# Cross attention: the keys of a tile are projected a step ahead, and VectorE rotates first in a step

## The chip, the cores and the metric

The kernel runs on one core of one Trainium2 chip. The metric is the device time of one execution in microseconds (us), here the median of several runs. PE is TensorE, PEld its weight loads, DVE VectorE, ACT ScalarE, POOL GpSimd, SP the engine that issues most of the DMAs.

## What is computed

A decoder layer on 16 sequences of 112 tokens, width 512, in float32: self attention, cross attention over 375 context tokens and the 112 of the sequence itself, and a mixture of experts. The change lies in the cross attention, which does this (cut from the reference):

```python
kv_in = jnp.concatenate([context_hidden, draft_hidden], axis=1)      # 375 + 112 = 487 rows
k = (kv_in @ Wk.T).reshape(bsz, total_len, KVH, HD)                  # 4 key heads of 128
v = (kv_in @ Wv.T).reshape(bsz, total_len, KVH, HD).transpose(0, 2, 1, 3)
k = _rms_norm(k, k_norm_w).transpose(0, 2, 1, 3)
q = _rope(q, draft_position_ids)
k = _rope(k, full_position_ids)
k = jnp.repeat(k, N_REP, axis=1)                                     # 16 query heads, 4 to a key head
scores = jnp.einsum('bhqd,bhkd->bhqk', q, k) * SCALE
probs = jax.nn.softmax(scores, axis=-1)
attn = jnp.einsum('bhqk,bhkd->bhqd', probs, v)
```

## The kernel before

`cross_attention` is one block in which each engine runs a program of its own, its order written out by hand; semaphores tie the programs together. `wait(eng, event, b, n)` holds an engine until the n-th event of batch b has happened. The 487 rows of keys and values are handled as four tiles i = 0 to 3: three of 125 context rows, one of the 112 rows of the sequence. The 16 query heads are four groups i = 0 to 3 of four heads j, one to a key head. So a batch is four *steps*, and step (b, i) does two things at once: the softmax of group i of batch b, and the projection of tile i of batch b + 1.

TensorE's operations are `score` (L2030, one head's scores into `ca_ps_s`, two buffers), `weigh` (L2046, probabilities times values of the group in front, into `ca_ps_o`), `keys` and `values` (`mm3`, L75 to L77, 12 matmuls each in three-part precision, into `ca_ps_p`), `turn` (L2037, four transposes of a head's probabilities into `ca_ps_t`) and `turn_k` (L2021, four transposes of a tile's finished keys into `ca_ps_r`).

Projected keys go through four engines. ScalarE squares them (`square`, L2092). VectorE multiplies them with the tables of sine and cosine (`rotate`, L2188 and L2191) into `k1` and `k2`, and sums the squares (`squares`, L2198, L2201). GpSimd adds the two products (L1958), takes the power -1/2 of the mean square (L1960) and scales the keys (L1964), and then makes the low part of the next context tile (`low`, L1952; ScalarE's `high`, L2085, makes the high part). TensorE turns the keys, and ScalarE copies them to `kT` (`keep_k`, L2097). The `keys` of a tile wait for its low part and for the rotation of the tile in front, the `rotate` for the turning of the tile in front.

The softmax of a head is `score`, `maximum` (VectorE, L2206), `exp` (ScalarE, L2112), `divide` (VectorE, L2211 and L2213), `turn`, `copy_pT` (ScalarE, L2119) and, in the next step, `weigh` and `copy_o` (ScalarE, L2124). The first score of a batch waits for `kT` of all four tiles.

`batches` runs `start` four times for the first batch (the preparation, with nothing beside it), then `step` 64 times, of which the last four (b = 15) project nothing. Steps of batches 2 to 13 are a hardware loop. `more` says that there is a next batch to project. The DMAs of the stage are SP's: `load` (x and tables of batch b + 2), `load_ctx` (context, L1891, once the low part of the last tile is made), `load_q` and `store`.

Of the kernel before, what the change touches and what calls it, by code (L numbers as in the profile page):

```python
# [1771 lines left out]
def cross_attention(nc, ahead_of, ctxT, xT_hi, xT_lo, tables, qT_src, oT):  # L1772
# [6 lines left out]
    with ctx:  # L1779
# [84 lines left out]
        def begun(b, i):  # L1864

            return not isinstance(b, int) or b or i

        def before(b, i):

            return (b, i - 1) if i else (b - 1, 3)

        @block.sync
        def _(sp):
            for i in range(2):
                o_put[i].open(sp)

            def load(b, h, par):
                cols = bass.ds(b * S, S)
                if not isinstance(b, int) or b > 1:  # L1880
                    wait(sp, v_mm, b, -5)
                    carry(sp, b, ticks)
                    wait(sp, k_rot, b, -5)
                    carry(sp, b, ticks)
                sp.dma_start(xh[par][:, :, :].bitcast(F32), xT_hi[:, :, cols]).then_inc(x_in[par].sem, 16)
                sp.dma_start(xl[par][:, :, :].bitcast(F32), xT_lo[:, :, cols]).then_inc(x_in[par].sem, 16)
                sp.dma_start(tab[par][:, :, :, :], tables[b]).then_inc(tab_in[par].sem, 16)

            def load_ctx(b):
                wait(sp, c_lo_ready, b, -1)  # L1890
                sp.dma_start(c_raw[:, :, :], ctxT[b]).then_inc(c_in.sem, 16)  # L1891

            def load_q(b, i):
                if not isinstance(b, int) or b or i > 1:
                    wait(sp, scored, b, (i - 1) * HQ - 1)
                sp.dma_start(qT[i % 2][:, :, :], qT_src[:, i * HQ:(i + 1) * HQ, bass.ds(b * S, S)])\
                    .then_inc(q_in[i % 2].sem, 16)

            def store(b, i):
                wait(sp, o_ready, b, i)  # L1900
                carry(sp, b, ticks)
                sp.dma_start(oT[:, i * HQ:(i + 1) * HQ, bass.ds(b * S, S)], ov[i % 2][:, :, :])\
                    .then_inc(o_put[i % 2].sem, 16)

            def body(b, h, par, first=False, more=1):

                load_q(b, 2)
                if not first:
                    store(b - 1, 3)  # L1910
                if more > 1:
                    load(b + 2, h + 1, par)
                load_q(b, 3)
                store(b, 0)
                if more > 1:
                    load_ctx(b + 2)
                if more:
                    load_q(b + 1, 0)
                store(b, 1)
                if more:  # L1920
                    load_q(b + 1, 1)
                store(b, 2)

            load(0, 0, 0)
            load_q(0, 0)
            load_q(0, 1)
            load(1, 0, 1)
            load_ctx(1)
            body(0, 0, 0, first=True, more=2)
            body(1, 0, 1, more=2)  # L1930
            with sp.Fori(1, B // 2 - 1) as h:
                for par in range(2):
                    body(h * 2 + par, h, par, more=2)
            body(B - 2, B // 2 - 1, 0, more=1)
            body(B - 1, B // 2 - 1, 1, more=0)
            store(B - 1, 3)
            for i in range(2):
                sp.wait_ge(o_put[i].sem, o_put[i].at(B - 1, 1))
# [39 lines left out]
        def _(pe):  # L1978
# [13 lines left out]
            def keys(b, h, i, par):  # L1992
                if first(b) and i == 0:
                    pe.wait_ge(w_lo_ready, 1)
                m, a_hi, a_lo = operands(b, i, par)
                if i == 3:
                    wait(pe, x_in[par], h, 1)
                else:
                    wait(pe, c_lo_ready, b, i)
                wait(pe, k_rot, b, i - 1)  # L2000
                for k in range(KD):
                    mm = mm3(pe, ps_p[0][0:m, :], a_hi[:, k, :], a_lo[:, k, :], w_hi[:, 0, k, :], w_lo[:, 0, k, :],
                             k == 0, k == KD - 1)
                mm.then_inc(k_mm.sem, 1)

            def values(b, i, par):
                if first(b) and i == 0:
                    pe.wait_ge(w_lo_ready, 2)
                m, a_hi, a_lo = operands(b, i, par)
                wait(pe, v_ready, b, i - 1)  # L2010
                for k in range(KD):
                    mm = mm3(pe, ps_p[1][0:m, :], a_hi[:, k, :], a_lo[:, k, :], w_hi[:, 1, k, :], w_lo[:, 1, k, :],
                             k == 0, k == KD - 1)
                mm.then_inc(v_mm.sem, 1)

            def turn_k(b, i):
                m = M[i]
                wait(pe, k_normed, b, i)
                wait(pe, kT_ready, b, i - 1)
                for j in range(KVH):  # L2020
                    mm = pe.transpose(ps_r[:, j * m:(j + 1) * m], k1[0:m, j * HD:(j + 1) * HD], ident[0:m, 0:m])  # L2021
                mm.then_inc(k_turned.sem, 1)
# [17 lines left out]
            def weigh(b, i, par):  # L2040
# [6 lines left out]
                                   start=(t == 0), stop=(t == 3))  # L2047
                mm.then_inc(pv.sem, 1)

            def start(b, i, par):  # L2050
                keys(b, 0, i, par)
                values(b, i, par)
                turn_k(b, i)

            def step(b, h, i, par, more):
                score(b, h, i, 0, par)
                score(b, h, i, 1, par)
                if begun(b, i):
                    pb, pi = before(b, i)
                    weigh(pb, pi, par if i else 1 - par)  # L2060
                if more:
                    keys(b + 1, h + par, i, 1 - par)
                turn(b, i, 0)
                turn(b, i, 1)
                score(b, h, i, 2, par)
                score(b, h, i, 3, par)
                if more:
                    values(b + 1, i, 1 - par)
                turn(b, i, 2)
                turn(b, i, 3)  # L2070
                if more:
                    turn_k(b + 1, i)

            batches(pe, start, step)
            weigh(B - 1, 3, 1)

        @block.scalar
        def _(act):
# [7 lines left out]
                    .then_inc(c_hi_ready.sem, 1)  # L2086

            def square(b, i):
                m = M[i]
                wait(act, k_mm, b, i)  # L2090
                wait(act, k_sum, b, 2 * i - 2)
                act.activation(sq[0:m, :], ps_p[0][0:m, :], ACT.Square).then_inc(k_sq.sem, 1)  # L2092
# [8 lines left out]
            def keep_v(b, i, par):  # L2101
                m = M[i]
                wait(act, v_mm, b, i)
                if not isinstance(b, int) or b > 1:
                    wait(act, pv, b, -5)
                act.activation(v[par][0:m, i, :], ps_p[1][0:m, :], ACT.Copy).then_inc(v_ready.sem, 1)
# [25 lines left out]
            def split(n):  # L2132
                act.wait_ge(w_in[n], 16)
                act.activation(w_hi[:, n, :, :], w_raw[:, n, :, :], ACT.Copy).then_inc(w_hi_ready, 1)

            def start(b, i, par):
                square(b, i)
                next_high(b, i, par)
                keep_v(b, i, par)
                keep_k(b, i, par)  # L2140

            def step(b, h, i, par, more):
                nb, npar = b + 1, 1 - par
                exp(b, i, 0)
                exp(b, i, 1)
                if begun(b, i):
                    copy_o(*before(b, i))
                if more:
                    square(nb, i)
                copy_pT(b, i, 0)  # L2150
                copy_pT(b, i, 1)
                exp(b, i, 2)
                exp(b, i, 3)
                if more:
                    keep_v(nb, i, npar)
                    next_high(nb, i, npar)
                copy_pT(b, i, 2)
                copy_pT(b, i, 3)
                if more:
                    keep_k(nb, i, npar)  # L2160

            k_sq.open(act)
            kT_ready.open(act)
# [4 lines left out]
            split(0)  # L2168
            high(0, 0, 0)
            split(1)  # L2170
            batches(act, start, step)
            copy_o(B - 1, 3)

        @block.vector
        def _(dve):
# [46 lines left out]
                squares(b, i)  # L2222

            def step(b, h, i, par, more):
                maximum(b, i, 0)
                maximum(b, i, 1)
                divide(b, i, 0)
                divide(b, i, 1)
                if more:
                    rotate(b + 1, h + par, i, 1 - par)  # L2230
                maximum(b, i, 2)
                maximum(b, i, 3)
                if more:
                    squares(b + 1, i)
                divide(b, i, 2)
                divide(b, i, 3)

# [489 lines left out]
```

## Time and profile before

| what | value |
|---|---|
| median of 3 runs | 2579.57 us (2574.31 to 2584.58) |
| the profiled execution | 2563.0 us, of which the span from first to last instruction is 2561.3 us |
| mean granted clock of TensorE | 0.941 of full speed |
| busy over the span | PE 86%, PEld 65%, DVE 52%, ACT 40%, POOL 31% |
| first score of the cross attention | at 1074.0 us |
| last score of the cross attention | at 1999.1 us |

The shares are means over stages with different limits, so the stage from some 1030 to 2005 us is read by itself.
### The profile page before, as it was taken

The numbers are of one execution on the slowest core, as the hardware profiler recorded it, in microseconds if no ns is written. First come the engines' busy times: TensorE is split into PE (matmuls) and PEld (weight loads), VectorE is DVE, ScalarE is ACT, GpSimd is POOL, SyncE is SP. The second block draws the span as 40 slices with busy tenths as digits, with TensorE's granted clock in tenths as the row PEclk, the third lists the DMA queues.
The fourth block names the chain that finished last, engine by engine and source line by source line (L and its number), as shares of the span: only waits on it lengthen the run. The fifth ranks groups of instructions, "written<-read, shape, count | busy, mean of one in ns | idle before, by whom it ended". The sixth has DMA issues, their size and how long they took to land. (4 is left out here: it accounts for less than half of the span.)

```text
span 2561.3 us, 35639 instructions
## 1 busy us (share of the span) xinstructions
PE 2201.1 (86%) x10448; PEld 1668.9 (65%) x10448; DVE 1333.2 (52%) x2902; ACT 1032.6 (40%) x2200; POOL 787.7 (31%) x818
## 2 busy tenths in 40 slices
PE   5699999975999986799999999999999799839991
PEld 3588888854777765566666666666665577627771
DVE  3535555547666766344444444444444555535553
ACT  2323333324434444244544544444455422125660
POOL 2400000004455556322322322322331011136664
PEclk9899999987999998799999999999999899959996
DMA  7621221142444444222222211222221533235336
GB/s 278 167 69 37 66 64 33 37 174 71 131 136 119 125 131 154 62 63 57 64 68 56 63 56 56 63 56 56 61 58 37 161 103 98 62 137 177 107 100 193
DMA packets 291586, 243.77 MB, mean 95 GB/s; under 512 B 148034, under 2 KB 255026, under 8 KB 288562
## 3 DMA queue, kind: packets, MB, share of 16 engines
q1 hardware_dynamic: 271426, 194.38, 25.6%
q10 hardware_dynamic: 13584, 30.02, 3.2%
q0 software_dynamic: 6496, 18.37, 2.6%
q8 instruction: 41, 0.67, 0.1%
q14 instruction: 39, 0.32, 0.0%
HBM read 149.31 MB, written 93.42 MB: 95 GB/s over the span
## 5 line engine op out<-in xcount | busy, mean ns | idle before, releaser
L2206 DVE TENSOR_REDUCE ca_down<-ca_ps_s 112x1 f32<-112x487 f32 x256 | 164.6, 661 | 210.6 <-PE ca_ps_s L2030 207.9
L1958 POOL TENSOR_TENSOR ca_k<-ca_k 125x512 f32<-125x512 f32 x64 | 82.5, 1290 | 606.8 <-DVE ca_k L2191 606.8
L2030 PE MATMUL ca_ps_s<-ca_kT,ca_qT 128*112 128x487 f32 x512 | 233.3, 577 | 13.0 <-ACT ca_kT L2097 10.0
L2112 ACT ACTIVATE ca_prob<-ca_ps_s,ca_down 112x487 f32<-112x487 f32 x256 | 169.7, 666 | 151.7 <-DVE ca_down L2206 147.7
L75 PE MATMUL out_ps_y<-out_w_hi,out_o_hi 128*128 128x512 f32 x448 | 190.6, 425 | 36.4 <-DVE out_w_lo L1288 18.4
L2046 PE MATMUL ca_ps_o<-ca_pT,ca_v 125*128 125x448 f32 (+1 forms) x512 | 203.2, 539 | 0.6 <-ACT ca_pT L2119 0.6
L75 PE MATMUL ca_ps_p<-ca_w_hi,ca_c_hi 128*125 128x512 f32 x384 | 187.6, 489 | 12.3 <-POOL ca_c_lo L1952 12.3
L2188 DVE TENSOR_TENSOR ca_k<-ca_ps_p,ca_tab 125x512 f32<-125x512 f32 x64 | 44.3, 692 | 289.0 <-ACT ca_sq L2092 289.0
L76 PE MATMUL out_ps_y<-out_w_lo,out_o_hi 128*128 128x512 f32 x448 | 183.2, 409 | 0.0
L77 PE MATMUL out_ps_y<-out_w_hi,out_o_lo 128*128 128x512 f32 x448 | 182.5, 407 | 0.0
L2046 PEld LDWEIGHTS ca_ps_o<-ca_pT,ca_v 125*128 125x128 f32 (+1 forms) x512 | 97.2, 190 | 100.9 <-issue 100.1
L77 PE MATMUL ca_ps_p<-ca_w_hi,ca_c_lo 128*125 128x512 f32 x384 | 153.7, 400 | 0.0
L76 PE MATMUL ca_ps_p<-ca_w_lo,ca_c_hi 128*125 128x512 f32 x384 | 153.5, 400 | 0.0
L2037 PEld LDWEIGHTS ca_ps_t<-ca_ident,ca_prob 112*125 112x125 f32 x1024 | 131.8, 188 | 23.1 <-DVE ca_prob L2213 10.2
L599 POOL COPY sa_val<-lat_v 112x128 f32<-112x128 f32 (+1 forms) x64 | 18.7, 294 | 411.0 <-PE sa_ps_o L656 410.7
L2037 PE MATMUL ca_ps_t<-ca_ident,ca_prob 112*125 112x112 f32 x1024 | 132.7, 272 | 6.3 <-DVE ca_prob L2213 5.7
L2030 PEld LDWEIGHTS ca_ps_s<-ca_kT,ca_qT 128*112 128x112 f32 x512 | 81.0, 177 | 76.4 <-issue 76.4
L75 PEld LDWEIGHTS out_ps_y<-out_w_hi,out_o_hi 128*128 128x128 f32 x448 | 89.8, 200 | 59.1 <-issue 33.1
L2119 ACT ACTIVATE ca_pT<-ca_ps_t 125x448 f32<-125x448 f32 x256 | 125.0, 544 | 3.8 <-PE ca_ps_t L2037 3.8
L2213 DVE TENSOR_SCALAR ca_prob<-ca_prob,ca_inv 112x487 f32<-112x487 f32 x256 | 121.2, 474 | 9.0
L75 PE MATMUL sa_ps_q<-sa_xh,qf_hi 128*128 128x448 f32 (+1 forms) x256 | 115.7, 452 | 8.5 <-DMA sa_xl<-x0T_lo 8.5
L707 ACT ACTIVATE sa_ov<-sa_ps_o 128x448 f32<-128x448 f32 x64 | 34.9, 546 | 194.8 <-PE sa_ps_o L656 187.8
(291 smaller groups left out, 5603.1 us busy)
## 6 DMA issues: line engine op xcount, KB each, us to landing
self_outT<-sa_ov SPq DMA_DIRECT2D x64, 224.0 KB, 2.4
out_o_raw<-self_outT SPq DMA_DIRECT2D x56, 256.0 KB, 3.0
cross_qT<-out_qt SPq DMA_DIRECT2D x56, 256.0 KB, 2.5
ca_qT<-cross_qT SPq DMA_DIRECT2D x64, 224.0 KB, 2.8
cross_outT<-ca_ov SPq DMA_DIRECT2D x64, 224.0 KB, 3.0
out_o_raw<-cross_outT SPq DMA_DIRECT2D x56, 256.0 KB, 3.1
ffn_raw<-in_expert_w SPq DMA_DIRECT2D x8, 1536.0 KB, 6.8
ca_c_first<-in_ctxT SPq DMA_DIRECT2D x15, 750.0 KB, 4.2
```

The source lines that it names most:

```text
L75: pe.matmul(out, a_hi, b_hi, start=start, stop=False)
L76: pe.matmul(out, a_hi, b_lo, start=False, stop=False)
L77: return pe.matmul(out, a_lo, b_hi, start=False, stop=stop)
L1958: pool.tensor_tensor(k1[0:m, :], k1[0:m, :], k2[0:m, :], ALU.add).then_inc(k_added.sem, 1)
L2030: pe.matmul(ps_s[j % 2][:, :], qT[i % 2][:, j, :], kT[par][:, i, :], start=True, stop=True).then_inc(scored.sem, 1)
L2037: mm = pe.transpose(ps_t[j % 2][0:CT, t, :], prob[j][:, t * CT:(t + 1) * CT], ident[0:S, 0:S])
L2046: mm = pe.matmul(ps_o[:, :, :], v[par][0:M[t], t, i * HD:(i + 1) * HD], pT[i % 2][0:M[t], t, :, :], start=(t == 0), stop=(t == 3))
L2112: act.activation(prob[j][:, 0:KV], ps_s[j % 2][:, :], ACT.Exp, bias=down[:, j:j + 1], accum_out=total[:, j:j + 1]).then_inc(exped.sem, 1)
L2119: act.activation(pT[i % 2][0:CT, :, j, :], ps_t[j % 2][0:CT, :, :], ACT.Copy).then_inc(pT_ready.sem, 1)
L2188: dve.tensor_tensor(h4(k1[0:m, :]), h4(ps), over_heads(tab[par][0:m, i, 0, :], HQ), ALU.mult)
L2206: dve.tensor_reduce(down[:, j:j + 1], ps_s[j % 2][:, :], AX.X, ALU.max, negate=True).then_inc(maxed.sem, 1)
L2213: dve.tensor_scalar(prob[j][:, 0:KV], prob[j][:, 0:KV], inv[:, j:j + 1], None, ALU.mult).then_inc(probs.sem, 1)
```

## The change

In a step TensorE now does the `values` where it did the `keys`, turns the keys right behind the scores of heads 2 and 3, and projects the keys of the tile that is turned in the *next* step (`next_keys`) in front of the last two `turn`s. ScalarE's and VectorE's programs follow: `square` moves behind `keep_k` in the second half, `rotate` to the front of the step, `squares` between the maxima and the divisions of the first half. `further` says whether there is a tile left for `next_keys`.

```diff
+        def further(b, i):
+            return not isinstance(b, int) or b + (2 if i == 3 else 1) < B
...
+            def next_keys(b, h, i, par):
+                if i < 3:
+                    keys(b, h, i + 1, par)
+                else:
+                    keys(b + 1, h + par, 0, 1 - par)
+
             def start(b, i, par):
-                keys(b, 0, i, par)
                 values(b, i, par)
+                next_keys(b, 0, i, par)
                 turn_k(b, i)
 
             def step(b, h, i, par, more):
...
                     weigh(pb, pi, par if i else 1 - par)
                 if more:
-                    keys(b + 1, h + par, i, 1 - par)
+                    values(b + 1, i, 1 - par)
                 turn(b, i, 0)
                 turn(b, i, 1)
                 score(b, h, i, 2, par)
                 score(b, h, i, 3, par)
                 if more:
-                    values(b + 1, i, 1 - par)
+                    turn_k(b + 1, i)
+                if further(b, i):
+                    next_keys(b + 1, h + par, i, 1 - par)
                 turn(b, i, 2)
                 turn(b, i, 3)
-                if more:
-                    turn_k(b + 1, i)
-
+
+            keys(0, 0, 0, 0)
             batches(pe, start, step)
...
             def square(b, i):
-                m = M[i]
+                m = M[i % 4]
...
             def start(b, i, par):
-                square(b, i)
                 next_high(b, i, par)
                 keep_v(b, i, par)
+                square(b, i + 1)
                 keep_k(b, i, par)
 
             def step(b, h, i, par, more):
                 nb, npar = b + 1, 1 - par
                 exp(b, i, 0)
                 exp(b, i, 1)
+                if more:
+                    next_high(nb, i, npar)
                 if begun(b, i):
                     copy_o(*before(b, i))
                 if more:
-                    square(nb, i)
+                    keep_v(nb, i, npar)
                 copy_pT(b, i, 0)
                 copy_pT(b, i, 1)
                 exp(b, i, 2)
                 exp(b, i, 3)
                 if more:
-                    keep_v(nb, i, npar)
-                    next_high(nb, i, npar)
+                    keep_k(nb, i, npar)
+                if further(b, i):
+                    square(nb, i + 1)
                 copy_pT(b, i, 2)
                 copy_pT(b, i, 3)
-                if more:
-                    keep_k(nb, i, npar)
...
+            square(0, 0)
             batches(act, start, step)
...
             def step(b, h, i, par, more):
+                if more:
+                    rotate(b + 1, h + par, i, 1 - par)
                 maximum(b, i, 0)
                 maximum(b, i, 1)
+                if more:
+                    squares(b + 1, i)
                 divide(b, i, 0)
                 divide(b, i, 1)
-                if more:
-                    rotate(b + 1, h + par, i, 1 - par)
                 maximum(b, i, 2)
                 maximum(b, i, 3)
-                if more:
-                    squares(b + 1, i)
                 divide(b, i, 2)
                 divide(b, i, 3)
```

## Rows read from the trace of the kernel before

**Rows 1.** Stretches of the preparation and of one batch: length, busy time of each engine.

```profile
core 0: us, PE busy (x) PEld busy (x) DVE busy (x) ACT busy (x) POOL busy (x), PEclk, DMA share, GB/s
1026.00:1074.00 48.00, 33.18 (x112) 24.25 (x112) 15.20 (x22) 9.89 (x17) 18.95 (x16) 0.78 0.18 57
1133.00:1192.00 59.00, 57.23 (x241) 38.11 (x241) 27.94 (x68) 29.11 (x67) 17.23 (x15) 1.00 0.23 61
```

**Rows 2.** Waits of TensorE's matmuls, 1074 to 1962: total us, times, longest.

```profile
PE ca_ps_r L2021 <- POOL ca_k L1964: 19.4, 60, 0.6
PE ca_ps_s L2030 <- ACT ca_kT L2097: 10.0, 12, 0.9
```

**Rows 3.** Waits of all engines, 1074 to 1962: the weight loads' one.

```profile
PEld ca_ps_r L2021 <- POOL ca_k L1964: 30.1, 60, 0.7
```

**Rows 4.** Time line of the weight loads through one step.

```profile
1502.98 0.28 PEld L2030 LDWEIGHTS ca_ps_s<-ca_kT,ca_qT 128*112 128x112 f32 x2
...
1504.32 0.19 PEld L2046 LDWEIGHTS ca_ps_o<-ca_pT,ca_v 125*128 125x128 f32 x1 [0.24 <-issue]
...
1507.36 0.19 PEld L75 LDWEIGHTS ca_ps_p<-ca_w_hi,ca_c_hi 128*125 128x125 f32 x1 [0.19 <-issue]
...
1510.28 1.07 PEld L2037 LDWEIGHTS ca_ps_t<-ca_ident,ca_prob 112*125 112x125 f32 x8
1511.28 0.28 PEld L2030 LDWEIGHTS ca_ps_s<-ca_kT,ca_qT 128*112 128x112 f32 x2
...
1512.60 0.19 PEld L75 LDWEIGHTS ca_ps_p<-ca_w_hi,ca_c_hi 128*125 128x125 f32 x1 [0.23 <-issue]
1513.02 0.18 PEld L76 LDWEIGHTS ca_ps_p<-ca_w_lo,ca_c_hi 128*125 128x125 f32 x1 [0.23 <-issue]
...
1515.56 1.07 PEld L2037 LDWEIGHTS ca_ps_t<-ca_ident,ca_prob 112*125 112x125 f32 x8
1517.11 0.41 PEld L2021 LDWEIGHTS ca_ps_r<-ca_ident,ca_k 125*128 125x128 f32 x4 [0.48 <-POOL ca_k L1964]
1517.49 0.28 PEld L2030 LDWEIGHTS ca_ps_s<-ca_kT,ca_qT 128*112 128x112 f32 x2
```

**Rows 5.** The same at the boundary of two batches.

```profile
1486.78 0.39 PEld L2021 LDWEIGHTS ca_ps_r<-ca_ident,ca_k 112*128 112x128 f32 x4 [0.46 <-POOL ca_k L1964]
1488.21 0.27 PEld L2030 LDWEIGHTS ca_ps_s<-ca_kT,ca_qT 128*112 128x112 f32 x2 [1.04 <-issue]
```

**Rows 6.** The same: first loads of step (0, 0) and of step (15, 0).

```profile
1074.04 0.45 PEld L2030 LDWEIGHTS ca_ps_s<-ca_kT,ca_qT 128*112 128x112 f32 x2 [0.86 <-issue]
...
1961.99 0.27 PEld L2030 LDWEIGHTS ca_ps_s<-ca_kT,ca_qT 128*112 128x112 f32 x2 [0.86 <-issue]
```

**Rows 7.** Time line of the other engines in the step of rows 4.

```profile
1504.11 0.67 DVE L2206 TENSOR_REDUCE ca_down<-ca_ps_s 112x1 f32<-112x487 f32 x1 [2.79 <-PE ca_ps_s L2030]
...
1506.61 0.47 DVE L2213 TENSOR_SCALAR ca_prob<-ca_prob,ca_inv 112x487 f32<-112x487 f32 x1
...
1510.79 0.60 ACT L2092 ACTIVATE ca_sq<-ca_ps_p 125x512 f32<-125x512 f32 x1 [2.21 <-PE ca_ps_p L77]
...
1511.28 0.97 ACT L2119 ACTIVATE ca_pT<-ca_ps_t 125x448 f32<-125x448 f32 x2
...
1511.42 0.69 DVE L2188 TENSOR_TENSOR ca_k<-ca_ps_p,ca_tab 125x512 f32<-125x512 f32 x1 [4.33 <-ACT ca_sq L2092]
...
1512.69 1.23 DVE L2206 TENSOR_REDUCE ca_down<-ca_ps_s 112x1 f32<-112x487 f32 x2
1512.85 1.28 POOL L1958 TENSOR_TENSOR ca_k<-ca_k 125x512 f32<-125x512 f32 x1 [9.19 <-DVE ca_k L2191]
...
1514.80 1.14 POOL L1960 TENSOR_TENSOR ca_k_rstd<-ca_ssum,ca_minus_half 125x4 f32<-125x4 f32 x1 [0.66 <-DVE ca_ssum L2201]
...
1516.01 1.04 POOL L1964 TENSOR_TENSOR ca_k<-ca_k,ca_k_rstd 125x512 f32<-125x512 f32 x1
...
1517.17 1.16 POOL L1952 TENSOR_TENSOR ca_c_lo<-ca_c_first,ca_c_hi 128x500 fp32r<-128x500 f32 x1
```

**Rows 8.** Time line of the preparation: tile 2 is turned, tile 3 rotated.

```profile
1062.12 0.42 PEld L2021 LDWEIGHTS ca_ps_r<-ca_ident,ca_k 125*128 125x128 f32 x4 [3.31 <-POOL ca_k L1964]
...
1067.79 0.69 DVE L2188 TENSOR_TENSOR ca_k<-ca_ps_p,ca_tab 112x512 f32<-112x512 f32 x1 [7.93 <-ACT ca_sq L2092]
```

**Rows 9.** Time line of the matmuls in the last batch.

```profile
1970.83 1.51 PE L2037 MATMUL ca_ps_t<-ca_ident,ca_prob 112*125 112x112 f32 x8 [1.44 <-DVE ca_prob L2213]
```

## The prediction

> **What bounds the kernel now.** I read the table of stretches first, to see which engine fills the stage that the diff touches. In a stretch of one batch of the cross attention TensorE is busy 57.2 of 59.0 us at a granted clock of 1.00 (2.4 GHz), while VectorE, ScalarE and GpSimd are busy about half of it or less [rows 1]. So TensorE sets the time, and only its few idle moments can be won. The chain that ended last says nothing here: it covers only the end of the kernel.
>
> Next the waits of TensorE over the 60 steps that project a tile. As matmuls they come to 19.4 us before the turning of the keys (60 times, for GpSimd's scaled keys) and 10.0 us before the first score of a batch (12 times seen, for ScalarE's copy `kT`) [rows 2]. As weight loads the first is 30.1 us [rows 3]. The two do not agree, so I went to the weight loads in order of time, which show when each group is let in. I call the groups of a step S (scores), W (`weigh`), K (`keys`), V (`values`), T (`turn`), R (`turn_k`). Today's order is S W K T S V T R.
>
> From first load to first load of the next group [rows 4]: S 1.34 (1502.98 to 1504.32), W 3.04, K 2.92, T 1.00, S 1.32, V 2.96, T 1.55, R 0.38. The two T's do the same work, yet the one in front of R takes 0.55 us more, and 0.48 of that is shown as R's wait for `ca_k`. So the row hides some 0.07 us: unhindered, the next group's loads begin 1.00 us after T's first, not 1.07. At the batch boundary R to S takes 1.43 us (1486.78 to 1488.21) instead of 0.38 [rows 5]: 1.05 us for a wait shown as 0.83 among the matmuls.
>
> **Part 1: `turn_k` in the middle of the step, its keys projected a step earlier.** Take T's load in the second half as 0. Today ScalarE's square starts 0.51 behind T's load (1510.28 to 1510.79), VectorE's rotation 1.14 behind and is over at about 2.5; GpSimd then adds 1.28, takes the root 1.14, scales 1.04 and the keys are ready at about 6.8, or 17.05 on the clock of the rows; R follows at 17.11 [rows 4, 7]. In the new order K stands in front of the last T. Square at 0.51 and rotation 1.14 to 2.41 keep their distances, since VectorE has nothing in front of the rotation; the add is over at 3.75. VectorE then does two maxima (0.67 each) and the sum of squares (0.68 and 0.17 as row 7 prices neither: from the page of the time line) to 4.6, the root ends at 5.8, the scaling at 6.9. R now comes after T 1.00, S 1.33, W 3.04, V 2.92, T 1.00, S 1.32, that is 10.6 us. It has 3.7 us to spare, so R's wait goes: 60 times (0.50 + 0.07) = 34.2, from 30.1/60 = 0.50. I round to **35 us**, as the boundary steps hide a little more.
>
> **Part 2: `kT_ready` at the batch boundary.** `keep_k` of tile 3 now lies before K and T, over 3 us ahead of the next S. 15 boundaries (the first behind the preparation) times 1.05 us: **16 us**. Together 51 us.
>
> By the matmuls' idle time alone it would be 19.4 + 15 x 0.83 = 32 us. I take the 51, because start to start of the loads includes the refilling of the array. The Trainium skill, Perfetto Trace Analysis, section Identifying the Most-Contended Engine, says that matmul busy time is no good measure of the distance to the bound, since pipelined instructions look smaller in the trace; by that rule the smaller sum is the one to distrust, and the rows agree with it (1.05 against 0.83 us).
>
> **Part 3: new neighbours in TensorE's queue.** V behind W costs what K behind W costs, 2.92. R behind S must wait for S's last pass: 0.42 (as the first load of V behind S, 1512.60 to 1513.02) plus three loads at 0.10, 0.70. K behind R then has no long pass in front of it: 2.96 less (0.42 - 0.19) = 2.73 with a load of 0.19 bare, or 2.64 if it hides behind R. R + K is 3.34 to 3.43, against 0.38 + 2.96 = 3.34 for R and V today. Cost 0 to 0.09 us a step, 0 to 5.4 in all. No row shows this succession; nothing excludes a cost twice as large, nor a small gain of the 0.07 above. I take 0.045: **+2.7 us**.
>
> **Part 4: VectorE and ScalarE.** Rotating first delays the first maximum: its score comes 1.13 us behind S's load (1502.98 to 1504.11), 2.13 on the scale above, and VectorE is free at 2.41; the `squares` in front of `divide` add 0.85. `divide` 1 was over at 1507.08, 4.1 behind S's load; it moves to about 5.0, and T needs it 7.3 behind S's load. Cover 2.3 us, cost nothing; if the cover were gone each 0.1 us would be 6 us. In the second half the rotation and `squares` go away, so `divide` 2 and 3 come 0.3 to 1 us earlier, while T comes later. On ScalarE `next_high`, `copy_o`, `keep_v` lie under V; `keep_k` under K. The square lies in front of the last two `copy_pT`, as it does in the first half today, where they end 1.97 us behind T's load (1510.28 to 1512.25). W's load comes at 2.33. **The smallest cover is here, 0.36 us**, less the time of a semaphore. Today the second pair has `keep_v` and `high` in front, but R and its wait behind T.
>
> **Part 5: loads and GpSimd.** No DMA is added or moved, and SP's queue keeps its order. `low` follows the scaling and ends at about 8.1; K needs it at 11.3: 3.2 us to spare. The context of the next batch is requested when `low` of tile 2 is done, now some 8 us earlier in its step, and is needed two steps later. Cost nothing.
>
> **Part 6: the ends.** In the preparation each tile's chain of square, rotation, GpSimd and `low` sets the pace; K of tile 1 and 2 waits for `low` as before. K of tile 3 now overlaps GpSimd's work on tile 2: today the turning of tile 2 starts at 1062.12 and the rotation of tile 3 only at 1067.79 [rows 8]; with K already done it can start at about 1063, some 4.5 us earlier. Against that `turn_k` of tile 3 queues behind `low` (1.16) and K of the next batch (2.7 us, or up to twice that, since the mean granted clock of the preparation is 0.78 [rows 1]). Net -1 to +2, taken as +0.5. The last projecting step loses its K (2.7 us) and exposes the wait of T for `divide` as the last batch has it, 1.44 [rows 9]: -1.3.
>
> **Sum.** -35 - 16 + 2.7 + 0.5 - 1.3 = **-49 us**. Check: the 60 steps took 1961.99 - 1074.04 = 887.95 us [rows 6], 14.80 each; without waits a step is 1.33 + 3.04 + 2.92 + 1.00 + 1.32 + 3.34..3.43 + 1.00 = 13.95 to 14.04, or 837 to 842 for 60, which is 46 to 51 less. The profiled execution took 2563.0 us by its own time (span 2561.3), the median of the runs is 2579.57, 0.6% above; the saving is of the same work, so I carry it over: 2514 for a profile like this one, and **2530.5** as the median.
>
> **Rivals.** (a) *Only the visible idle time comes back*: the refilling is paid elsewhere, for example at R behind S. 32 - 5.4 gives about -27: 2553. For it: that succession is in no row. Against: the check of the sum. (b) *W takes over the wait*, as `copy_pT` comes late behind the square. If it is late by 0.4 us (0.36 of cover gone and as much again), 60 times, 24 of the 49 are lost: 2554. For it the thin cover; against it that the same three instructions take 1.97 us in the first half in every step seen. (c) *Nothing changes*, because a wait of full size appears elsewhere, such as T for `divide`: it needs VectorE 2.3 us later than worked out, and then 0.8 us a step: 2580. (d) *Slower*: GpSimd's chain becomes the bound. The loop K, square, rotation, add, root, scaling, `low`, next K is 2.7 + 8.1 = 10.8 us against 14.0. It stalls from +3.2 us, and is slower than today from +4.0. If GpSimd's four instructions (4.6 us) took double beside the maxima and divisions that they now fall on, the loop is 15.4 us, 0.6 above today: +37, 2616. Against: the add already runs beside maxima today in 1.28 us, the root beside divisions in 1.14.
>
> **How the numbers follow.** My forecast 0.75; (a) 0.09; (b) 0.07; (c) 0.05; (d) 0.03; 0.01 for more gain than forecast. Some 0.5% (13 us) is what a measurement can tell: the three runs lie from 2574.31 to 2584.58. Forecast, (a) and (b) lie beyond it: faster 0.92, same 0.05, slower 0.03. Forecast alone: 2520 to 2542 (Part 3 from -4 to +11, the ends 3, the runs 5). The range that holds 8 in 10 reaches down to 2518 and, to take in most of (a) and (b), up to 2552.
>
> **What would show it.** In the new profile: no wait of the matmuls of `ca_ps_r` for `ca_k`, nor of `ca_ps_s` for `ca_kT`; TensorE over 98% busy in a stretch of one batch at clock 1.00; steps of 14.0 us; R's load 0.42 us behind S's last, K's T 2.7 behind K. (b) would show as `ca_ps_o` waiting for `ca_pT`, (c) as `ca_ps_t` waiting for `ca_prob` in the steps that project, (d) as `ca_ps_p` waiting for `ca_c_lo`. The forecast is wrong if any of these is more than a few us, or if the granted clock of the stage falls below 1.00.

## The result, and the profile after

The changed kernel takes 2522.49 us (median of 5 runs, 2519.65 to 2526.26) against 2576.06 us (5 runs, 2572.50 to 2584.58): a ratio of 0.978, 95% interval 0.9764 to 0.9796. That is 53.6 us less by the medians; 49 were forecast, from 2579.57 us, the median of the first three runs, to 2530.5. The measured 2522.5 lies in the range of 2518 to 2552, 8.0 us below the forecast: 3.5 of them come from the base, which is lower with five runs, and the rest from the larger saving.

The first view is the stretch of one batch, which answers to [rows 1]. The columns are the length, the busy time of PE, PEld, DVE, ACT and POOL, then TensorE's granted clock.

```profile
1133.00:1192.00 59.00, 59.00 (x252) 39.77 (x251) 28.95 (x71) 30.01 (x69) 19.80 (x18) 1.00 0.23 62
```

TensorE is busy in all of the 59 us, at clock 1.00. The waits of its matmuls from 1077 to 1900 us, which were 19.4 us for `ca_k` and 10.0 us for `ca_kT` before [rows 2], are down to a single line:

```profile
PE ca_ps_s L2035 <- issue: 0.8, 1, 0.8
```

The time line of the weight loads through one step answers to [rows 4]. It begins with the T in front of the step, and only the first loads of the groups are shown.

```profile
1506.26 1.08 PEld L2042 LDWEIGHTS ca_ps_t<-ca_ident,ca_prob 112*125 112x125 f32 x8
1507.27 0.28 PEld L2035 LDWEIGHTS ca_ps_s<-ca_kT,ca_qT 128*112 128x112 f32 x2
...
1508.59 0.19 PEld L2051 LDWEIGHTS ca_ps_o<-ca_pT,ca_v 125*128 125x128 f32 x1 [0.23 <-issue]
...
1511.64 0.17 PEld L75 LDWEIGHTS ca_ps_p<-ca_w_hi,ca_xh 128*112 128x112 f32 x1 [0.19 <-issue]
...
1514.56 1.07 PEld L2042 LDWEIGHTS ca_ps_t<-ca_ident,ca_prob 112*125 112x125 f32 x8
1515.55 0.28 PEld L2035 LDWEIGHTS ca_ps_s<-ca_kT,ca_qT 128*112 128x112 f32 x2
...
1516.88 0.14 PEld L2026 LDWEIGHTS ca_ps_r<-ca_ident,ca_k 112*128 112x128 f32 x1 [0.23 <-issue]
1517.29 0.33 PEld L2026 LDWEIGHTS ca_ps_r<-ca_ident,ca_k 112*128 112x128 f32 x3 [0.27 <-issue]
1517.58 0.19 PEld L75 LDWEIGHTS ca_ps_p<-ca_w_hi,ca_c_hi 128*125 128x125 f32 x1
...
1520.24 1.08 PEld L2042 LDWEIGHTS ca_ps_t<-ca_ident,ca_prob 112*125 112x125 f32 x8
1521.23 0.28 PEld L2035 LDWEIGHTS ca_ps_s<-ca_kT,ca_qT 128*112 128x112 f32 x2
```

From S to S it is 13.96 us (1507.27 to 1521.23), against 14.51 in the step of [rows 4]. R's first load stands 0.41 us in front of the others, as it was let in under the last pass of S, and R and K together take 3.36 us here (1516.88 to 1520.24) and 3.38 in the mean of the 58 steps between the first and the last, against 0.38 + 2.96 for R and V before.

The other engines in the same step answer to [rows 7]:

```profile
1506.78 0.60 ACT L2104 ACTIVATE ca_sq<-ca_ps_p 112x512 f32<-112x512 f32 x1 [1.36 <-PE ca_ps_p L77]
...
1507.27 0.97 ACT L2131 ACTIVATE ca_pT<-ca_ps_t 125x448 f32<-125x448 f32 x2
1507.41 0.69 DVE L2202 TENSOR_TENSOR ca_k<-ca_ps_p,ca_tab 112x512 f32<-112x512 f32 x1 [1.76 <-ACT ca_sq L2104]
...
1509.82 0.68 DVE L2212 TENSOR_REDUCE ca_ssum<-ca_sq 112x4 f32<-112x512 f32 x1
...
1510.53 0.17 DVE L2215 TENSOR_SCALAR ca_ssum<-ca_ssum 112x4 f32<-112x4 f32 x1
...
1510.78 1.14 POOL L1965 TENSOR_TENSOR ca_k_rstd<-ca_ssum,ca_minus_half 112x4 f32<-112x4 f32 x1 [0.68 <-DVE ca_ssum L2215]
...
1512.00 1.04 POOL L1969 TENSOR_TENSOR ca_k<-ca_k,ca_k_rstd 112x512 f32<-112x512 f32 x1
...
1513.00 1.17 POOL L1957 TENSOR_TENSOR ca_c_lo<-ca_c_first,ca_c_hi 128x500 fp32r<-128x500 f32 x1
```

Behind T's first load at 1506.26 the square comes at 0.52, the rotation at 1.15, and the scaling ends at 6.8, `low` at 7.9. R is loaded at 10.6. GpSimd's root stands idle for 0.68 us until VectorE's sum of squares is there, which matters in experiments 4 and 7. (The 0.68 and 0.17 us that the prediction takes in Part 1 for the sum of squares and its scaling are the two VectorE lines in the middle.)

Last, the first loads of step (0, 0) and of step (15, 0), which answer to [rows 6]:

```profile
1076.54 0.27 PEld L2035 LDWEIGHTS ca_ps_s<-ca_kT,ca_qT 128*112 128x112 f32 x2 [0.96 <-issue]
...
1911.83 0.28 PEld L2035 LDWEIGHTS ca_ps_s<-ca_kT,ca_qT 128*112 128x112 f32 x2
```

The 60 steps took 835.3 us instead of 887.95, 52.7 less. From the first `keys` to the last `weigh` the stage takes 923.3 us (1029.78 to 1953.07) instead of 974.9 (1028.33 to 2003.22), 51.6 less. The profiled executions themselves are only 36.7 us apart (2563.0 and 2526.3), which the first experiment looks into.

### The profile page after: what moved, and what is told of

Its sections match the earlier page's. It is cut to its first block and busy times, and to the rows that moved or that the text cites. A ratio compares the mean times of both kernels' runs of the same rounds, so it can differ in the third digit from the quotient of the medians.

```text
span 2524.6 us, 35645 instructions
## 1 busy us (share of the span) xinstructions
PE 2182.0 (86%) x10448; PEld 1661.2 (66%) x10448; DVE 1332.6 (53%) x2902; ACT 1030.3 (41%) x2200; POOL 785.3 (31%) x818
## 5 line engine op out<-in xcount | busy, mean ns | idle before, releaser
L75 PE MATMUL ca_ps_p<-ca_w_hi,ca_c_hi 128*125 128x512 f32 x384 | 174.1, 453 | 23.1 <-POOL ca_c_lo L1957 23.1
```

What stands on the lines that cost most here:

```text
L75: pe.matmul(out, a_hi, b_hi, start=start, stop=False)
```

## The experiments

The base of all but the first is the changed kernel; times are medians. Experiments 1, 2, 3 and 8 shared 15 runs of the kernel before, 2575.45 us; experiments 4 to 7 shared 7, on another chip, 2569.93 us. So a difference of medians between one of 4 to 7 and the changed kernel (2522.49, beside 2576.06) may come out up to 6 us too small, and there the stage decides. The numbers of the stage come from the weight loads of each run's profile, read as above.

### 1. The kernel before once more

The unchanged kernel.

> The kernel before, unchanged, to learn what its profile varies by behind the cross attention. In the first profile the time from the last `weigh` (2003.22 us) to the end of the span was 558.1 us; in the changed kernel it was 571.5 us (2524.6 - 1953.07). Theory A: this is variation from execution to execution, since no instruction there changed; a second profile of the kernel before shows the cross attention again as 887.9 us from the first score of step (0, 0) to that of (15, 0), but the rest behind it some 5 to 15 us longer than 558. Rival B: the changed kernel leaves the stages behind in a worse state (clock), so the kernel before repeats 558 within 2 us.

2575.76 us, ratio 1.0001 (0.9987 to 1.0015). The two profiles of it agree in the stage to some hundredths: 974.87 us against 974.89, and these are the first loads of steps (0, 0) and (15, 0), 887.97 us apart:

```profile
1077.82 0.45 PEld L2030 LDWEIGHTS ca_ps_s<-ca_kT,ca_qT 128*112 128x112 f32 x2 [0.86 <-issue]
...
1965.79 0.27 PEld L2030 LDWEIGHTS ca_ps_s<-ca_kT,ca_qT 128*112 128x112 f32 x2 [0.86 <-issue]
```

What varies lies outside: from the last `weigh` to the end 558.1 us in the first profile and 560.3 in the second, and the first `keys` of the stage came at 1028.3 and at 1032.2. That is 2.2 us, less than the 5 to 15 of theory A and a little more than B's 2. The profiles of experiments 2 to 8, all of the changed kernel's kind, have 562.2 to 567.5 us behind the stage (565.9 and 567.5 in experiments 7 and 4), so the 571.5 of the changed kernel's profile is the longest end of all. Both profiles of the kernel before were fast executions of it (2563.0 and 2569.0 against a median of 2576), and the changed kernel's was the slowest of its five (2526.26). The medians show no cost behind the stage: less the stage, the kernel before leaves 1601.2 us (2576.06 - 974.89) and the changed kernel 1599.2 (2522.49 - 923.29). What makes an end long or short stays open. The saving is to be read from the stage (51.6) and from the medians (53.6), not from one pair of profiles (36.7).

### 2. `turn_k` back at the end of the step

```diff
-                if more:
-                    turn_k(b + 1, i)
                 if further(b, i):
                     next_keys(b + 1, h + par, i, 1 - par)
                 turn(b, i, 2)
                 turn(b, i, 3)
+                if more:
+                    turn_k(b + 1, i)
```

ScalarE's `keep_k` moves behind its last `copy_pT` as well.

> The changed kernel with `turn_k` back at the end of the step, behind the last two `turn`s, while the keys are still projected a step ahead. This keeps part 1 (the turning no longer waits for GpSimd, 35 us) and undoes part 2 (the wait for `kT` at the batch boundary). Theory A, loads counted start to start: 15 boundaries at 1.05 us, 16 us more than the changed kernel, some 2539 against 2522.5. Rival B, matmul idle time counted: 12 to 15 times 0.83, 10 to 12 us, 2534. Rival C: the boundary wait was only a consequence of the late keys and is gone with them, 2522. The step without boundary stays 14.0 us in A and B.

2542.05 us, ratio 0.9871 (0.9852 to 0.9891): 19.6 more than the changed kernel. Steps inside a batch take 14.0 us, the last of a batch 15.0 to 15.1. So the wait for `kT` is a cost of its own, not a consequence of the late keys, and it costs 1.0 to 1.15 us at a boundary. The matmuls' waits from 1080 to 1900 us show less:

```profile
PE ca_ps_s L2035 <- ACT ca_kT L2109: 10.8, 12, 0.9
```

That is 0.9 each. Theory A, with 16 us, is right, B with 10 to 12 and C with none are not. The stage as a whole is 22.7 us longer; of that 17.2 lie in the 60 steps and 0.8 in the preparation, which the edit doesn't touch and which took as much more in experiment 3. The rest, 4.7 us, is in the last batch: steps (15, 0) and (15, 1) took 13.23 and 11.67 us instead of 10.09. In the middle of the three stretches below, TensorE's granted clock is 0.69 in the mean, so part of it ran at 1.2 GHz; in the stretch in front of it TensorE had been busy 7.7 of 10 us. The median is only 19.6 us up, so the 4.7 need not be in every execution.

```profile
1921.50:1931.50 10.00, 7.73 (x38) 5.04 (x36) 3.18 (x9) 5.05 (x11) 1.69 (x2) 0.97 0.17 47
1931.50:1941.50 10.00, 9.97 (x24) 4.90 (x24) 2.85 (x7) 2.93 (x7) 0.00 (x0) 0.69 0.01 2
1941.50:1951.50 10.00, 8.43 (x27) 4.47 (x26) 4.78 (x12) 4.37 (x11) 0.00 (x0) 0.83 0.17 46
```

### 3. VectorE rotates behind the first two maxima

```diff
-                if more:
-                    rotate(b + 1, h + par, i, 1 - par)
                 maximum(b, i, 0)
                 maximum(b, i, 1)
                 if more:
+                    rotate(b + 1, h + par, i, 1 - par)
                     squares(b + 1, i)
```

> The changed kernel with VectorE's rotation behind the first two maxima instead of in front of them. Theory A: everything beside TensorE has 2 to 3.7 us to spare, so the place of the rotation within the first half is worth nothing: the keys are scaled some 1.3 us later, still 2.4 us ahead of their turning; same time within 3 us (2522). Rival B: rotating first is what takes the wait away; then the matmuls of the turning wait again and some 0.3 to 0.6 us a step come back, 18 to 35 us.

2526.85 us, ratio 0.9807 (0.9787 to 0.9826): 4.4 more, a little over the 3 of theory A, with overlapping intervals. In the stage it is 2.4 us: the steps are 14.0 us as before and no matmul of the turning waits. Of the 2.4, 0.8 are in the preparation, untouched by the edit, and 1.6 in step (0, 0): there no `weigh` stands in front of the first T, which comes so much sooner and waits 1.2 us for the division that the rotation has delayed. In the steady steps the place of the rotation within the first half is worth nothing.

### 4. VectorE in the order of the kernel before

```diff
-                if more:
-                    rotate(b + 1, h + par, i, 1 - par)
                 maximum(b, i, 0)
                 maximum(b, i, 1)
-                if more:
-                    squares(b + 1, i)
                 divide(b, i, 0)
                 divide(b, i, 1)
+                if more:
+                    rotate(b + 1, h + par, i, 1 - par)
                 maximum(b, i, 2)
                 maximum(b, i, 3)
+                if more:
+                    squares(b + 1, i)
```

> The changed kernel with VectorE in the order of the kernel before: rotation behind the first two divisions, sum of squares behind the last two maxima. Theory A (the worked-out times): the sum of squares then ends about 11.6 us behind the load of the last `turn`, the root at 12.8, the scaling at 13.9, and the turning, due at 10.6, waits 3.2 us or a little more in every step: a step of 17.2 to 17.5 us, 190 to 210 us more than the changed kernel, some 2720; slower than the kernel before. Rival B: VectorE's order is a detail and the gain is TensorE's new order; within 10 us of 2522.

2905.36 us, ratio 1.1303 (1.1277 to 1.1328): 383 us more than the changed kernel, and 383.9 in the stage, twice what theory A gave. B is out: TensorE's new order without VectorE's is slower than the kernel before by 335 us. The loads of one step show both parts of the excess:

```profile
1511.27 0.28 PEld L2035 LDWEIGHTS ca_ps_s<-ca_kT,ca_qT 128*112 128x112 f32 x2
...
1517.06 0.41 PEld L2026 LDWEIGHTS ca_ps_r<-ca_ident,ca_k 125*128 125x128 f32 x4 [4.70 <-POOL ca_k L1969]
1518.24 0.18 PEld L75 LDWEIGHTS ca_ps_p<-ca_w_hi,ca_c_hi 128*125 128x125 f32 x1 [0.77 <-issue]
1519.03 0.33 PEld L75 LDWEIGHTS ca_ps_p<-ca_w_hi,ca_c_hi 128*125 128x125 f32 x1
```

S to R takes 5.79 us instead of 1.33, a wait of 4.5 where I had 3.2; I had the sum of squares too early, as it stands behind two maxima that wait for the second pair of scores. The other engines in this step show that this sum is what GpSimd waits for:

```profile
1508.42 1.30 POOL L1963 TENSOR_TENSOR ca_k<-ca_k 125x512 f32<-125x512 f32 x1 [11.00 <-DVE ca_k L2205]
...
1513.79 0.68 DVE L2212 TENSOR_REDUCE ca_ssum<-ca_sq 125x4 f32<-125x512 f32 x1
...
1514.75 1.14 POOL L1965 TENSOR_TENSOR ca_k_rstd<-ca_ssum,ca_minus_half 125x4 f32<-125x4 f32 x1 [5.03 <-DVE ca_ssum L2215]
```

The rotation is over by 1508.35 and the add by 1509.72; GpSimd then stands idle for 5.03 us until the sum of squares is there. Had that sum followed the late rotation at once, root and scaling (1.14 and 1.04 us) would, by these times, have been over at some 1512, before R was due at 1512.60. That is an estimate; the two moves were not run apart.

Behind the idle time the loads take 0.33 us instead of 0.18, and K takes 4.22 us here (1518.24 to 1522.46) instead of 2.66, and 4.0 to 4.9 in 56 of the 58 steps between the first and the last. The stretches of the same step, 2 us each, say why: the granted clock is 1.00 through the idle time and 0.64 and 0.51 behind it, that is the 1.2 GHz level.

```profile
1512.00:1514.00 2.00, 1.17 (x3) 0.18 (x1) 1.46 (x3) 1.02 (x4) 0.00 (x0) 1.00 0.00 0
1514.00:1516.00 2.00, 0.00 (x0) 0.00 (x0) 1.74 (x6) 0.66 (x2) 1.18 (x2) 1.00 0.81 198
1516.00:1518.00 2.00, 0.65 (x4) 0.41 (x4) 0.00 (x0) 0.26 (x1) 2.00 (x2) 1.00 0.11 32
1518.00:1520.00 2.00, 1.75 (x5) 1.39 (x6) 0.00 (x0) 0.34 (x1) 0.12 (x1) 0.64 0.44 69
1520.00:1522.00 2.00, 2.00 (x7) 1.52 (x6) 0.00 (x0) 0.00 (x0) 0.00 (x0) 0.51 0.79 312
1522.00:1524.00 2.00, 2.00 (x14) 1.63 (x13) 0.00 (x0) 1.03 (x3) 0.00 (x0) 1.00 0.01 3
```

A step is 20.4 us in the mean of those 58: 14.0, plus 4.5 of wait in front of R, plus 0.3 between R and K, where K waits for `low`, plus 1.7 of K at the lower clock.

### 5. Each square made twice

```diff
+                act.activation(sq2[0:m, :], ps_p[0][0:m, :], ACT.Square)
                 act.activation(sq[0:m, :], ps_p[0][0:m, :], ACT.Square).then_inc(k_sq.sem, 1)
```

> The changed kernel, in which ScalarE makes each square twice (once into a spare tile), 0.49 us more in front of the last two `copy_pT` of a step. It measures the thinnest cover: the copies end 0.35 us before the load of `weigh` in the profile. Theory A: the cover is real and all there is, so `weigh` starts 0.14 us late plus a semaphore and the refilling, 0.15 to 0.3 us a step: 9 to 18 us more, and 2 in the preparation, some 2536, with `ca_ps_o` waiting for `ca_pT`. Rival B: there is more room than start times show; 2 us more, 2524.

2524.76 us, ratio 0.9818 (0.9797 to 0.9840). Against its own base that is 45.2 us less where the changed kernel has 53.6; in the stage it is 4.6 more, 2.9 in the preparation and 1.7 in step (15, 1), whose clock fell. In the steps B is right, nothing is lost: the 60 take 835.3 us, exactly as without the second square. And yet `weigh` comes late, by 0.1 to 0.26 us in every one behind the first. In this one the last T is loaded at 1445.17 and the copies end at 1447.64:

```profile
1446.26 1.80 PE L2035 MATMUL ca_ps_s<-ca_kT,ca_qT 128*112 128x487 f32 x4
...
1446.65 0.99 ACT L2132 ACTIVATE ca_pT<-ca_ps_t 125x448 f32<-125x448 f32 x2
...
1447.76 0.33 PEld L2051 LDWEIGHTS ca_ps_o<-ca_pT,ca_v 125*128 125x128 f32 x2 [0.50 <-issue]
1448.28 0.19 PEld L2051 LDWEIGHTS ca_ps_o<-ca_pT,ca_v 125*128 125x128 f32 x1 [0.19 <-issue]
```

The first load of W comes 2.59 us behind T's instead of 2.33, so 0.26 late; but the second follows it at once instead of 0.41 behind, and W is over in 2.78 us instead of 3.05. The matmuls of S in front run on to 1448.06 by the trace (1446.26 + 1.80, a modelled end), so even the late load is taken in under the last of them. The Trainium skill (TensorE: Matmul & The Clock Gate, Part 2: What happens when you issue a matmul) says that weight loads are pulled ahead of matmuls in flight, while the matmuls stay in order. The trace agrees, with W's first load at 1447.76, still under S. So the cover at `weigh` was not the 0.36 us that I took from start times, but at least 0.62 (0.36 + 0.26).

### 6 and 7. GpSimd given two and four extra additions a tile

```diff
+                for r in range(2):          # 4 in experiment 7
+                    pool.tensor_tensor(k3[0:m, :], k1[0:m, :], k2[0:m, :], ALU.add).then_inc(more_adds.sem, 1)
+                    wait(pool, more_adds, b, i * 2 + r)
                 pool.tensor_tensor(k1[0:m, :], k1[0:m, :], k2[0:m, :], ALU.add).then_inc(k_added.sem, 1)
```

> The changed kernel with two extra additions of the same size (1.28 us each, into a spare tile, each waited for) on GpSimd in front of the real one, 2.7 us more a tile. It tests the room of GpSimd's chain. Theory A: the turning has 3.7 us to spare and the next keys 3.2, so the steps stay 14.0 us and only the preparation grows, by 4 times 2.7: some 11 us, 2533. Rival B: GpSimd's chain is nearly the bound; 0.5 us a step or more, over 30 us besides.

> The same with four extra additions, 5.4 us more a tile. Theory A: the turning now waits 5.4 - 3.7 = 1.7 us and the next keys wait until 2.2 us behind their due time, so a step is about 16.1 us: 2.1 times 60 = 126 us more, and 22 in the preparation, some 2670, with the waits at `ca_ps_r` and `ca_ps_p` L75. Rival B, no bound at all from GpSimd: 22 us more.

With two: 2530.30 us, ratio 0.9844 (0.9822 to 0.9866), 7.8 more by the medians and 11.2 in the stage, where 11 were expected. The steps stay at 14.0 us (836.4 for the 60, of which the 1.1 more are in step (0, 0)), the preparation grows by 10.2. With four, one run, so its time has no interval: 2618.9 us. The 60 steps take 908.5 us, 73.2 more or 1.2 a step, and the preparation 22.2 more. Theory A is right on where the room ends, but had 2.1 us a step, since it let the chain grow by the full 5.4 us. The scaling ends 11.5 us behind T's first load here instead of 6.8, which is 4.7 later: the root waited 0.68 us for the sum of squares in the changed kernel, and the first part of the additions falls into that wait. With two additions it ends 8.8 behind, 2.0 later. With 4.7, R is 0.9 us late, which puts its room at 3.8 us, as forecast:

```profile
1502.45 0.28 PEld L2039 LDWEIGHTS ca_ps_s<-ca_kT,ca_qT 128*112 128x112 f32 x2
...
1504.67 0.41 PEld L2030 LDWEIGHTS ca_ps_r<-ca_ident,ca_k 125*128 125x128 f32 x4 [1.13 <-POOL ca_k L1973]
```

S to R is 2.22 us here instead of 1.33. Where the next keys are those of a context tile, in three steps of four, R to K is 1.1 to 1.2 us instead of 0.7 as well, as K waits for `low`. The clock stays at 1.00. So the slower case (d) of the prediction is real and lies where it was put: not reached with 2.0 us more in the chain; with 4.7 a step is 15.1 us in the mean, more than the 14.80 of the kernel before.

The additions also slow VectorE beside them, so this is not quite a test of GpSimd alone: the scaling of the sum of squares (L2219) takes 0.95 us in the mean of both experiments instead of 0.17, and a division's multiplication (L2231) up to 1.50 instead of 0.47. In step (0, 0) of both experiments T waits for a division, 0.6 to 0.7 us as matmuls.

### 8. Another preparation

```diff
             low(0, 0, 0)
+            low(0, 1, 0)
...
+                if isinstance(b, int) and b == 0:
+                    if i == 0:
+                        low(0, 2, 0)
+                    elif i == 2:
+                        low(1, 0, 1)
-                if i in (0, 1):
+                elif i in (0, 1):
                     low(b, i + 1, par)
```

and the same for ScalarE's `high`.

> The changed kernel with another preparation: the high and low parts of context tile 1 are made at once, those of tile 2 behind the first tile's keys, and those of the next batch's tile 0 a tile earlier, so that the keys of the next tile are projected while GpSimd works on the one in front. Nothing else changes. Theory A: the preparation is bound by the chain square, rotation, add, root, scaling, `low`, keys, 12 us a tile for tiles 1 and 2 in the profile (keys start at 1029.8, 1041.2, 1053.5; first score at 1076.5). With K outside that chain a tile takes about 6 us: 12 to 18 us less, some 2507. Rival B: TensorE at its lower clock in the preparation (0.78 of full speed in the mean before) needs 10 us a tile for K and V anyway, so less than 5 us are won.

2507.50 us (5 runs, 2501.31 to 2513.78), ratio 0.9740 (0.9722 to 0.9758) to the kernel before: the fastest of all, 15.0 us less than the changed kernel. From the first `keys` to the first score it takes 29.7 us instead of 46.8, and the turning of the four tiles shows the pace, 5.8 to 6.1 us each:

```profile
1041.39 0.41 PEld L2032 LDWEIGHTS ca_ps_r<-ca_ident,ca_k 125*128 125x128 f32 x4 [0.58 <-POOL ca_k L1969]
...
1047.20 0.58 PEld L2032 LDWEIGHTS ca_ps_r<-ca_ident,ca_k 125*128 125x128 f32 x4
...
1053.28 0.49 PEld L2032 LDWEIGHTS ca_ps_r<-ca_ident,ca_k 125*128 125x128 f32 x4
...
1059.27 0.47 PEld L2032 LDWEIGHTS ca_ps_r<-ca_ident,ca_k 112*128 112x128 f32 x4
```

B falls too: TensorE is busy 29.1 of 30 us there, and its mean clock is 0.94, against 0.82 in the changed kernel's preparation (1030 to 1076 us).

## Why the prediction was right

**Parts 1 and 2, the two waits, 51 us.** Both are gone from the profile. The two accounts differed by a factor of 1.6: 32 us by the matmuls' idle time, 51 by the loads, start to start. The 60 steps took 52.7 us less, of which some 2.9 belong to the clock (see the sum below); the rest decides for the second account. Load by load, T to R took 1.58 us in the mean before and T to S takes 0.99 now, 35.2 us over 60 steps, against 35. The last steps of the batches give the other 15 to 16. Experiment 2 shows the same for the boundary alone (1.0 to 1.15 us against 0.9 of matmul idle time). Rival (a) is out. The wait behind the preparation stays (1.52 us from R to S); the 15 boundaries are those behind it.

**Part 3, R behind S and K behind R.** Forecast 3.34 to 3.43 us for the pair, measured 3.38 in the mean; against 3.34 before it cost 2.2 us of the 2.7 taken.

**Part 4, VectorE and ScalarE.** The times worked out for the new order held to 0.2 us (scaling over at 6.9, measured 6.8). The step that was mis-sized is the thinnest cover: 0.36 us was the distance of start times, and experiment 5 shows that 0.26 us beyond it still cost nothing. Rival (b) was further off than I gave it. That VectorE's new order has room to spare is true within the first half (experiment 3), and false beyond: left as it was, it would have made the kernel slower than before (experiment 4). The trace of that run names the sum of squares, not the rotation, as what came too late. The prediction costed VectorE's new order at nothing and did not say that the gain hangs on it.

**Part 5, GpSimd and loads.** 3.7 us of room for the turning and 3.2 for the next keys; experiment 7 puts the first at 3.8, and 2.0 us more in the chain cost the steady steps nothing (experiment 6). No wait for `ca_c_lo` is left in the steps.

**Part 6, the ends.** The preparation grew by 1.05 us (45.71 to 46.76 from first `keys` to first score), forecast 0.5; the same preparation took 47.3 to 47.5 us in experiments 2 to 4. Both halves are as forecast: the rotation of tile 3 follows the load of tile 2's turning after 0.96 us instead of 5.67, and K of the next batch, in front of the last R, takes 4.14 us instead of 2.7. The last projecting step took 12.87 us, 1.1 less than 14.0, forecast 1.3.

**The sum.** The stage lost 51.6 us, the forecast had 49. Most of the difference is step (0, 0), which took 10.99 us instead of 14.32. It has no `weigh`, so 3.05 of a step's time is missing in both, and what the kernel before paid on top was the lower clock: its first S and K took 2.57 and 4.62 us, the changed kernel's S and V 1.32 and 2.96, which is 2.9 of the 3.3. Its mean granted clock is 0.67 from 1070 to 1080 us.

```profile
1070.00:1080.00 10.00, 6.53 (x15) 3.78 (x16) 3.03 (x7) 3.87 (x7) 3.66 (x4) 0.67 0.00 0
```

In the changed kernel, `keys` of the next batch stands in front of the last turning of the preparation, and the clock is 1.00 from 1076 to 1086 us. I take that place of `keys` to be why the clock was up in time; it was not tested by itself, and the prediction has no term for it, so that this part of the gain is luck.

**What the medians add**, 2 us beyond the stage, is within their spread; the stages in front and behind vary by more from one execution to the next.

## What to carry to other kernels

Where one engine is nearly always busy, count its waits from start to start of the weight loads and compare with the same pair of groups where nothing waits; the idle time of the matmuls gave 32 us here for waits that were worth 51. A chain through four engines is hidden by starting it a step earlier only if each of these engines serves it in time: here the new order of TensorE and ScalarE with VectorE's old one cost 335 us, and together with VectorE's new one it won 53. The head of the queue isn't needed (experiment 3); what must not happen is that a link of the chain, here the sum of squares, stands behind work that waits for something late. When the steady step is full, look at the preparation: 15 us by the medians and 17.1 in the stage were left there, in the moment at which the high and low parts of three tiles are made.

## What the runs showed that I had not expected

Behind waits of 4.5 us TensorE's clock was at its lower level in nearly every step, and the matmuls there paid another 1.7 us (experiment 4). Even in the last batch, where the waits of the matmuls are about 1.4 us, steps ran at the lower clock in four of the ten profiles, those of experiments 2, 4, 5 and 7, and cost 1.0 to 4.7 us, while in the changed kernel's profile the same steps ran at 10.09 us each. Why it fell in some executions and not in others stays open. A weight load that comes 0.26 us late costs nothing if the matmul in front still runs (experiment 5). And the stage repeated to 0.02 us between two executions, while the rest of the kernel varied by several us: differences of single profiles are to be taken stage by stage.
